# A transformer layer on one core: the tail of the token stage in a new order, and two edits ahead of it

## The reference

```python
x = x + attn(layernorm(x))     # Nystrom attention, 16 heads of 64, 64 landmarks, 6 pseudo-inverse rounds,
                               # a 13-tap convolution along the tokens, output weights w_fc, bias b_fc
x = x + moe(layernorm(x))      # sparsemixer router, top 2 of 8 experts, hidden size 512
...
sim1, sim2, sim3 = q @ k_l.T, q_l @ k_l.T, q_l @ k.T
out = softmax(sim1) @ pinv(softmax(sim2)) @ (softmax(sim3) @ v)
out = out + conv(out)          # along tokens, one filter of 13 taps per head
out = out @ w_fc + b_fc
...
h = silu(x @ w_gate[e].T) * (x @ w_up[e].T)
out = out + dense_w[:, e:e+1] * (h @ w_down[e].T)
```

## Time and profile before

| | us |
|---|---|
| median of 3 runs | 1186.02 (1185.68 to 1186.12) |
| profiled execution, whole | 1188.56 |
| its span, first to last instruction | 1186.8 |
| TensorE busy in it | 1122.7 (95%) |
| VectorE, ScalarE, GpSimd busy | 571.7, 301.7, 301.8 |
| mean granted TensorE clock | 0.991 of full speed |

### The profile page before, as it was taken

How to read it: one execution, slowest core, us unless ns; L and a number is a source line. 1 busy time by engine, 2 the same in 40 slices (tenths; PEclk the granted TensorE clock), 3 DMA queues, 4 the chain that set the end, 5 groups by cost and what they waited for, 6 DMA issues and landing times.

```text
span 1186.8 us, 22648 instructions
## 1 busy us (share of the span) xinstructions
PE 1122.7 (95%) x9066; PEld 886.9 (75%) x9066; DVE 571.7 (48%) x1273; ACT 301.7 (25%) x513; POOL 301.8 (25%) x298
## 2 busy tenths in 40 slices
PE   3999999999987899999999999878999999999997
PEld 3866667666776756677767766767888888899996
DVE  6254243232256557667777676654233323334442
ACT  4532222222223423223332332321111111111110
POOL 6000000000020003225435534443322332234343
PEclk9999999999999999999999999889999999999999
DMA  9300000000210030312321213235223332221221
GB/s 334 135 1 1 1 1 1 1 1 1 55 40 5 4 142 10 108 50 68 117 82 63 99 60 124 85 99 145 45 48 52 50 49 48 43 41 38 45 23 15
DMA packets 48551, 69.12 MB, mean 58 GB/s; under 512 B 7872, under 2 KB 41792, under 8 KB 47424
## 3 DMA queue, kind: packets, MB, share of 16 engines
q1 hardware_dynamic: 34720, 47.50, 12.5%
q0 software_dynamic: 13296, 16.92, 8.1%
q10 hardware_dynamic: 432, 3.24, 0.7%
HBM read 42.10 MB, written 26.46 MB: 58 GB/s over the span
## 4 chain that ended last, share of the span: by engine, by line
PE 89%; DVE 4%; issue 3%; POOL 1%; ACT 1%; another core or an unknown queue 1%; POOLq 0%; DVEq 0%; ACTq 0%
PE ps L1585 20%; PE ps L1608 10%; PE ps L1470 10%; PE ps L1268 9%; PE ps L1248 9%; PE ps L1509 9%; PE ps L1501 5%; PE ps L1259 3%; PE ps L1382 2%; PE ps L1211 1%; PE ps L1568 1%; PE ps L1489 1%; PE ps L1455 1%; PE ps L1223 1%
## 5 line engine op out<-in xcount | busy, mean ns | idle before, releaser
L1585 PE MATMUL ps<-mem 128*128 128x256 f32 (+1 forms) x1504 | 260.4, 329 | 0.0
L1585 PEld LDWEIGHTS ps<-mem 128*128 128x128 f32 x1504 | 232.6, 191 | 21.3
L554 POOL DMA_INDIRECT out<-mem x71 | 124.6, 1755 | 253.8 <-DVE mem L1130 188.0
L1608 PE MATMUL ps<-mem 128*128 x568 | 137.2, 385 | 5.0 <-DVE mem L1122 3.4
L524 POOL TENSOR_TENSOR mem<-mem,small 128x1024 f32<-128x1024 f32 x36 | 68.6, 1904 | 248.9 <-DVE small L1059 115.9
L1470 PE MATMUL ps<-mem 128*128 128x512 f32 x288 | 129.7, 594 | 1.3 <-DVE mem L943 1.3
L1122 DVE TENSOR_TENSOR mem<-mem,ps 128x512 f32<-128x512 f32 x71 | 48.8, 687 | 170.5 <-PE ps L1585 143.1
L742 ACT ACTIVATE mem<-ps 128x512 f32<-128x512 f32 x71 | 42.4, 597 | 322.6 <-PE ps L1585 315.8
L1509 PE MATMUL ps<-mem 128*128 128x256 f32 x512 | 119.7, 387 | 0.0
L1608 PEld LDWEIGHTS ps<-mem 128*128 128x128 f32 x568 | 105.6, 193 | 18.3 <-issue 5.7
L1248 PE MATMUL ps<-mem 128*128 128x512 f32 x256 | 115.4, 593 | 0.0
(11 more groups left out here) (205 smaller groups left out, 1316.2 us busy)
## 6 DMA issues: line engine op xcount, KB each, us to landing
mem<-w_gu SPq DMA_DIRECT2D x9, 1024.0 KB, 4.3
mem<-xs_d SPq DMA_DIRECT2D x22, 260.0 KB, 2.9
mem<-x SPq DMA_DIRECT2D x8, 512.0 KB, 7.4
mem<-x SPq DMA_DIRECT2D x32, 128.0 KB, 2.2
out<-mem SPq DMA_DIRECT2D x32, 128.0 KB, 1.7
mem<-w_down SPq DMA_DIRECT2D x8, 512.0 KB, 5.7
xnt_d<-mem ACTq DMA_DIRECT2D x3, 1056.0 KB, 4.4
mem<-xnt_d SPq DMA_DIRECT2D x3, 1056.0 KB, 4.9
```

The lines of the kernel that those rows point to most:

```text
L554: pool.indirect_dma_start(out=out_rows, out_offset=bass.IndirectOffsetOnAxis(ap=rows[:, D + 1:D + 2].bitcast(U32), axis=0), in_=ys[:, r % ...
L1585: mm = pe.matmul(bank(2 * c + n % 2)[:, i * size:(i + 1) * size], w[:, k, c, f * P:(f + 1) * P], xst[:, a % 2, k, 0:size], start=(k == 0), ...
L1608: mm = pe.matmul(bank(down_bank(a, b))[:, 0:D], hid[:, u, i * size + b * P:i * size + (b + 1) * P], w_d_s[:, e, f], start=(f == 0), stop=( ...
```

## The change

Five edits.

1. ACT_ROWS becomes a list per batch: ScalarE normalises tiles 3, 5, 7 of batches 0 and 1, tile 7 of batch 2 and none of batch 3. VectorE does the others. `act_rows` and `dve_rows` count them for the waits. ScalarE starts with a one-column ACTIVATE.
2. In batch 3 the last chunk's two products are copied out by VectorE, not by ScalarE.
3. The w_fc products of every second head pair are written to the opposite half of the output, so that a round's products use four quadrants, not two. The copy L943 reads them accordingly, and `c2_conv` places heads 2 and 3 of every four on opposite column halves, to match.
4. The tail's order on TensorE, ScalarE and VectorE. `x_columns(0)` moves into step 35, `hidden(0, 0)` and `hidden(1, 0)` in between the last convolutions; groups 6 to 8 are chosen and placed between the early items' work.
5. ScalarE gets two small ACTIVATEs of Exp in the tail (`exp_table`).

```diff
--- before.py
+++ after.py
-ACT_ROWS = (2, 5, 7)
+ACT_ROWS = ((3, 5, 7), (3, 5, 7), (7,), ())
...
+def act_rows(b, until=0):
+    return sum(len(rows) for rows in ACT_ROWS[:b]) + sum(t < until for t in ACT_ROWS[min(b, B - 1)])
+def dve_rows(b, until=0):
+    return RT * b + until - act_rows(b, until)
...
             act.wait_ge(s("a_consts"), 1)
+            act.activation(zz[:, 6:7], ident[:, 0:1], ACT.Identity, bias=ident[:, 1:2], scale=ident[:, 2:3])
...
-                for t in ACT_ROWS:
+                for t in ACT_ROWS[b]:
...
+                    if b == B - 1 and n == len(CHUNKS) - 1:
+                        act.wait_ge(s("a_xnt_dve"), 2 * KD)
+                        continue
...
-            for i in range(QT + 2):
+            def exp_table():
+                act.activation(zz[:, 7:8], zz[:, 1:2], ACT.Exp, scale=0.0)
+            for i in range(QT):
                 for h in range(2):
                     for g in groups_at(DONE, i - 2 - h):
                         if 2 * h < GROUPS[g][1]:
                             norm_columns(g, h)
-                if QT <= i < QT + 2:
-                    conv_out(i - 2)
                 for g in groups_at(CHOSEN, i - 1):
                     gap_exponentials(g)
                 for g in groups_at(DONE, i - 1):
                     for v in range(GROUPS[g][1]):
                         norm_rows(g, v)
-                if 2 <= i < QT:
+                if i >= 2:
                     conv_out(i - 2)
-                if i < QT:
-                    exponentials(i)
+                exponentials(i)
+            rows_transposed(0)
+            norm_columns(NG - 3, 0)
+            conv_out(QT - 2)
+            norm_columns(NG - 3, 1)
+            gate_out(0)
+            conv_out(QT - 1)
+            norm_rows(NG - 2, 0)
+            norm_rows(NG - 2, 1)
+            exp_table()
+            gap_exponentials(NG - 3)
             norm_columns(NG - 2, 0)
-            gap_exponentials(NG - 3)
-            rows_transposed(0)
             gap_exponentials(NG - 2)
-            gate_out(0)
+            gate_out(1)
+            rows_transposed(1)
             norm_rows(NG - 1, 0)
             norm_rows(NG - 1, 1)
-            gate_out(1)
             norm_columns(NG - 1, 0)
-            rows_transposed(1)
+            gate_out(2)
+            exp_table()
             gap_exponentials(NG - 1)
-            gate_out(2)
+            rows_transposed(2)
             gate_out(3)
-            rows_transposed(2)
             gate_out(4)
             rows_transposed(3)
...
+            ts = CHUNKS[-1]
+            for k in range(KD):
+                c = 6 * B - KD + k
+                dve.wait_ge(s("a_tp"), c + 1)
+                product = bank(c % 8)[:, 0:len(ts) * (P + RT)].rearrange("p (t c) -> p t c", t=len(ts))
+                at_ = HALO + P * ts[0]
+                dve.tensor_copy(xnts[B - 1][:, k, at_:at_ + P * len(ts)].rearrange("p (t c) -> p t c", t=len(ts)),
+                                product[:, :, 0:P]).then_inc(s("a_xnt_dve"), 1)
+                lm = M * (B - 1) + RT * ts[0]
+                dve.tensor_copy(xm[:, k, lm:lm + RT * len(ts)].rearrange("p (t c) -> p t c", t=len(ts)),
+                                product[:, :, P:P + RT]).then_inc(s("a_xnt_dve"), 1)
...
-                dve.tensor_copy(pm[:, g // 2, 4 * (g % 2):4 * (g % 2) + 4],
-                                bank(2 + 2 * (g % 2), 2).rearrange("p (s c) -> p s c", s=4)).then_inc(s("p_pm"), 1)
+                dve.tensor_copy(pm[:, g // 2, 4 * (g % 2):4 * (g % 2) + 4].rearrange("p (s o) c -> p o s c", o=2),
+                                bank(2 + 2 * (g % 2), 2).rearrange("p (o s c) -> p o s c", o=2, s=2)).then_inc(s("p_pm"), 1)
...
-            for i in range(QT + 4):
+            for i in range(QT + 1):
                 token_step(i)
+            rows_out(MT - 3)
+            statistics(MT - 3, NG - 2)
+            inverse_deviations(NG - 2)
             dve.wait_ge(s("c2_a1"), QT)
             hidden_out(0)
+            choices(NG - 3)
+            rows_out(MT - 2)
+            statistics(MT - 2, NG - 1)
+            slots(NG - 3)
+            choices(NG - 2)
+            rows_out(MT - 1)
+            statistics(MT - 1, NG - 1)
+            inverse_deviations(NG - 1)
+            hidden_out(1)
             slots(NG - 2)
-            hidden_out(1)
             choices(NG - 1)
+            rows_weighed(0)
+            hidden_out(2)
             slots(NG - 1)
             sizes()
             table(2 * P, 0, 8, NU, u_eid, u_row, "d_units")
-            hidden_out(2)
-            rows_weighed(0)
...
-                    for r in halves:
-                        mm = pe.matmul(bank(2 + 2 * (g % 2), 2)[r, i * D:(i + 1) * D], wts[r, g % 2, i], wfc[r, q % J],
-                                       start=True, stop=True)
+                    to = bank(2 + 2 * (g % 2) + i % 2)[:, i // 2 * D:(i // 2 + 1) * D]
+                    for h, r in enumerate(halves):
+                        mm = pe.matmul(to[halves[(h + i) % 2]], wts[r, g % 2, i], wfc[r, q % J], start=True, stop=True)
...
-                    c = 64 * (h % 2)
+                    c = 64 * ((h + h // 2) % 2)
...
+                if i == QT - 1:
+                    x_columns(0)
...
-            for i in range(QT + 2):
+            for i in range(QT):
                 token_step(i)
-            last = QT + 2
-            c2_tp(NG - 2, 0)
-            pe.wait_ge(s("c2_cvt"), cvt_count(QT - 1))
-            bank6_read(last)
-            c2_lg(NG - 2, 0)
-            c2_counts(NG - 3)
-            x_columns(0)
-            c2_y(MT - 1)
+            pe.wait_ge(s("m_xst"), 1)
+            c2_tp(NG - 3, 0)
+            c2_conv(QT - 2)
+            c2_lg(NG - 3, 0)
+            bank6_read(QT)
+            c2_y(MT - 3)
+            c2_tp(NG - 3, 1)
             pe.wait_ge(s("e_w_in"), 16)
             pe.wait_ge(s("c2_sub"), QT)
             hidden(0, 0)
             hidden(1, 0)
-            c2_counts(NG - 2)
+            c2_conv(QT - 1)
+            c2_lg(NG - 3, 1)
+            bank6_read(QT + 1)
+            c2_y(MT - 2)
+            c2_tp(NG - 2, 0)
+            c2_counts(NG - 3)
+            pe.wait_ge(s("c2_cvt"), cvt_count(QT - 1))
+            c2_lg(NG - 2, 0)
+            bank6_read(QT + 2)
+            c2_y(MT - 1)
             pe.wait_ge(s("d_taken"), NG - 2)
             hidden(0, 1)
             hidden(1, 1)
+            c2_counts(NG - 2)
+            x_columns(1)
+            pe.wait_ge(s("wd_in"), 16 * E)
+            pe.wait_ge(s("c2_x1"), MT)
+            down(0)
+            pe.wait_ge(s("m_xst"), 2)
             c2_tp(NG - 1, 0)
-            pe.wait_ge(s("wd_in"), 16 * E)
-            down(0)
+            down(1)
             pe.wait_ge(s("d_taken"), NG - 1)
             c2_lg(NG - 1, 0)
-            x_columns(1)
-            down(1)
-            c2_counts(NG - 1)
             hidden(0, 2)
             hidden(1, 2)
+            c2_counts(NG - 1)
+            x_columns(2)
             hidden(0, 3)
-            x_columns(2)
+            hidden(1, 3)
             down(2)
-            hidden(1, 3)
             hidden(0, 4)
             down(3)
             hidden(1, 4)
```

More of the change, by code:

```diff
@@ L344, in _ @@
                          router_t.rearrange("(k p) e -> p k e", p=P)).then_inc(s("w_in"), 16)
-            sp.wait_ge(s("a_xn_dve"), (RT - len(ACT_ROWS)) * (B - 1))
-            sp.wait_ge(s("a_xn_act"), len(ACT_ROWS) * (B - 1))
+            sp.wait_ge(s("a_xn_dve"), dve_rows(B - 1))
+            sp.wait_ge(s("a_xn_act"), act_rows(B - 1))
             sp.dma_start(wfc, w_fc.rearrange("(j p) c -> p j c", p=P)).then_inc(s("w_in"), 16)
@@ L594, in columns_out @@
                 if b >= 1:
-                    act.wait_ge(s("a_xnt"), 12 * (b + 1))
+                    act.wait_ge(s("a_xnt"), 12 * (b + 1) - (2 * KD if b == B - 1 else 0))
                     act.dma_start(xnt_d[b].rearrange("p (k n) -> p k n", k=KD), xnts[b]).then_inc(s("a_xnt_out"), 16)
@@ L801, in normalise @@
                 for t in range(RT):
-                    if t not in ACT_ROWS:
+                    if t not in ACT_ROWS[b]:
                         dve.tensor_scalar(xna[:, b, t], xbs[b][:, t], mv[:, b, t, 0:1], rs[:, b, t:t + 1],
@@ L1203, in _ @@
                 for n, ts in enumerate(CHUNKS):
-                    pe.wait_ge(s("a_xn_dve"), (RT - len(ACT_ROWS)) * b + sum(t not in ACT_ROWS and t <= ts[-1] for t in range(RT)))
-                    pe.wait_ge(s("a_xn_act"), len(ACT_ROWS) * b + sum(t <= ts[-1] for t in ACT_ROWS))
+                    pe.wait_ge(s("a_xn_dve"), dve_rows(b, ts[-1] + 1))
+                    if act_rows(b, ts[-1] + 1):
+                        pe.wait_ge(s("a_xn_act"), act_rows(b, ts[-1] + 1))
                     for k in range(KD):
@@ L1213, in _ @@
                         mm.then_inc(s("a_tp"), 1)
-            pe.wait_ge(s("a_xnt"), 12 * B)
+            pe.wait_ge(s("a_xnt"), 12 * B - 2 * KD)
+            pe.wait_ge(s("a_xnt_dve"), 2 * KD)
```

(52 more changed lines are left out.)

## The result

The changed kernel took 1176.53 us in the median of 4 runs (1175.75 to 1181.21), the kernel before 1186.07 beside it (4 runs). The ratio is 0.9927, with a 95% interval of 0.990 to 0.9954. The forecast was 1164.1, in 1159 to 1172. The kernel is faster, by 9.5 us and not by 22.

What follows compares the result with a forecast made beforehand. TensorE, busy 1122.7 of 1186.8 us, was taken as the bound, gaining only where it waits or its products run slow. Savings of 4.0, 6.9 and 11 sum to 21.9: 1164.1 against a median of 1186.02, range 1159 to 1172.

Steps and rivals of the forecast that it cites:

- The first stage: Start of the kernel: moving ScalarE's rows and last copies to VectorE saves 4.0 us, range 3.0 to 4.4.
- The quadrants: Output-weight rounds: four quadrants run together, halving 1.77 us per round, 0.87 saved in each of eight rounds, 6.9.
- rival B: Output-weight rounds: quadrants don't overlap in the w_fc products, so only 15.0 us saved, 1171; chance 0.10.
- rivals E and F: Convolutions: E, halves in strict program order, 8 us, chance 0.05; F, pair's heads run serially, 65 more, chance 0.03.
- The tail: Token stage's end to expert stage's start: new order saves 11 us, between 4 and 16 by late signals returning.
- With two fifths, 5 us: **11: Tail: two fifths of the 12.1 us of late signals return, costing 5 us, so 11 is saved.
- late signals: Tail: three waits, 12.1 us in all, with unknown releaser, after TensorE's product had ended, while GpSimd scatters rows.
- rival C: Tail: the late signals return in full, so 14.9 us saved in all, 1171; chance 0.15.
- The working without late signals: Tail: regular expert items start at 802.2 instead of 818.34, 16 us saved if no signal is late.
- VectorE's list: Tail: VectorE sets the end after the change; its work there, without waits, takes 40.9 us.
- first fixed point: Tail: VectorE's `rows_out` at 756.76, released by GpSimd's bias, which the change doesn't move.
- Terms 1 and 2: First stage, 4.0 us saved by moved rows and copies; output-weight rounds, 6.9 us saved by four quadrants.

Runs made afterwards that it cites:

- e2: Kernel before with only the w_fc products in four quadrants and the convolution's halves in the new order: 1179.8 us, ratio 0.9949.
- e12: The changed kernel again, unchanged, on another chip: 1173.1 us, ratio 0.9904.
- e3: Kernel before with only the tail's new order and the two small Exp ACTIVATEs: 1183.5 us, ratio 0.9987.
- e9: Changed kernel with one semaphore increment and wait on GpSimd behind each scatter of all groups: 1172.7 us, ratio 0.9892.
- e14: Changed kernel with four pairs of semaphore increment and wait on GpSimd behind each scatter of groups 5 to 8: 1175.0 us, ratio 0.9915.
- e1: Kernel before with only the first stage's rows and last copies moved from ScalarE to VectorE: 1182.7 us, ratio 0.9968.
- e11: Kernel before with one semaphore increment and wait on GpSimd behind each scatter of all groups: 1187.5 us, ratio 1.0009.
- e17: Kernel before with the first-stage and quadrant edits, tail in its old order, repeated on another chip: 1171.1 us, ratio 0.9903.
- e18: The changed kernel again, unchanged, on a chip without held signals: 1168.8 us, ratio 0.9881.
- e6_pauses_all: Changed kernel with eight pairs of semaphore increment and wait on GpSimd behind each scatter of groups 5 to 8: 1164.2 us, ratio 0.9858.
- e10: Changed kernel with eight semaphore increments and no wait on GpSimd behind each scatter of groups 5 to 8: 1169.9 us, ratio 0.9864.
- e13: Changed kernel with 14 semaphore increments and no wait on GpSimd behind each scatter of groups 5 to 8: 1170.7 us, ratio 0.9878.
- e8: Kernel before with the first-stage and quadrant edits, tail in its old order, no pauses: 1171.8 us, ratio 0.9907.
- e5: Changed kernel with eight pairs of semaphore increment and wait on GpSimd behind each scatter of groups 6 to 8: 1166.4 us, ratio 0.9874.
- e7: Kernel before with first-stage and quadrant edits, old tail order, eight increment-and-wait pairs behind each scatter of groups 6 to 8: 1169.1 us, ratio 0.989.
- e15: Kernel before with eight pairs of semaphore increment and wait on GpSimd behind each scatter of groups 5 to 8: 1186.0 us, ratio 0.9998.
- e16: Changed kernel with eight increment-and-wait pairs behind every scatter and every addition of rows in the expert stage: 1173.0 us, ratio 0.9895.
- e4: Changed kernel with one more GpSimd sum of 0.73 us into unused memory behind each scatter of groups 6 to 8: 1173.6 us, ratio 0.9902.

## Why the prediction was wrong

**The first stage** was right: 4.36 against 4.0. TensorE's start gave 0.8, the rest is ScalarE's rows and the last copies.

**The quadrants** were right, in size and in reason: 0.86 per round, eight rounds, 6.86 against 6.9. Two quadrants that read through the same half of the array do overlap with 256 columns too; rival B falls. The convolution stayed at 1.81 in after and e2, so rivals E and F fall. From the rule of the Trainium skill, page "TensorE: Matmul & The Clock Gate", section "Part 3: Packing small matmuls", that MATMULs start and end strictly in program order, I had worked out the loss of a slot at each repeated half; the page doesn't state that loss, and this trace shows none. One of my reasons was weaker than it looked. Products of two lines start between each other in the pseudo-inverse because the program's loop calls them in turn, which says little of quadrants. In the trace of before their records start at most 0.13 us out of that order.

**The tail** is where it failed, at the sentence "With two fifths, 5 us: **11**". In the profiled execution all of the late signals returned, and more: 12.1 before, 15.0 after. That is rival C, at 0.15, and the result lies beyond even that. In e12, the same kernel, 7.2 stood and the tail was 440.5, still only 5.6 under that of before. The working without late signals was close: 16 saved from a tail of 446.1 is 430.1, and the tails with the new order and nothing held are 432.4, 432.3 and 433.4. Of that 16, though, 12.1 was never the order's to give. Old tails with nothing held are 434.9, 436.6 and 439.5, 4.3 more in the mean than the new ones; the forecast's own difference, 16 - 12.1, is 3.9. Nor does the time of late signals seem all lost: on the two chips without them the kernel before is only 3 to 4.5 faster, not 12, though it was not profiled there. Where signals are held, as in the runs that the forecast was made against, the new order shows 439.9 to 446.6 (after, e3, e9, e12, e14), the old one 441.0 to 446.1 (before, e1, e2, e11). The means are 441.9 and 444.2, with spreads of 5 to 7. So where signals are held the orders differ by 2.3, less than either spread; e3, the order alone, won 3.0 in the medians and 1.5 by the ratio, and its interval takes in no change. Of the reasons that I gave for a smaller share, "early items give TensorE work ahead of the points that wait" didn't carry. In after TensorE did its two `down` and then stood for 6.9, as the logits behind them wait for ScalarE, and ScalarE for the signal that was held. The signals of both `down`, one ahead of the transposes and one behind, came out together with theirs (779.8 to 780.65), so work placed around a held signal didn't shorten the hold. And the pause brought the lower clock, which my sum left to the range.

**VectorE's list** was near. The waits of VectorE in after, from 749.5 to 811, stand against the earlier trace rows; the first is the logits' product, late by the hold:

```profile
DVE mem L1016 <- PE ps L1535: 10.7, 1, 10.7
DVE mem L1155 <- issue: 2.8, 1, 2.8
...
DVE mem L1016 <- remote: 1.8, 1, 1.8
```

The work itself was near the forecast: 61.9 from its first fixed point, less the 18.2 of waits listed for it, is 43.7, and I had 40.9, with 1.15 for a register load and an issue gap. My count of TensorE's products up to group 8's logits was a slip: its parts add up to 29.4 and not 28.9, which makes 0.5. ScalarE's two extra table loads were hidden: the list of VectorE's waits in after names ScalarE nowhere.

**The sum.** Terms 1 and 2 give 11.2. The change won 13.2 on the chip of e17 and e18. On chips that hold signals it won 9.5 (the result) and 11.8 (e12), so there the tail gave between -1.7 and 0.6 where 11 was forecast, with the pseudo-inverse's scatter in it. The range of 1159 to 1172 was too narrow on this side. It took the holds as known from one execution. The kernel before alone spreads over 1178 to 1192 in 81 runs beside e1 to e18.

**The best version** so far is e6_pauses_all with 1164.2, 0.9858 of before, on a chip without held signals. After stands at 0.9881 on the other such chip, and the intervals overlap. Where signals are held, e10 and e13 (0.9864, 0.9878) stand under after (0.9904, 0.9927).

## What to carry to other kernels

A stall whose releaser the profile can't name doesn't belong to the order of the work. If its cause isn't known, forecast the gain once with it back in full and once without it, and keep both in the range. Sort a saving into what the edit does and what it hopes will vanish: here the first was 3.9 of 16. And run a control on the same chip before crediting a cure: e8 showed that e5 to e7 were no evidence of one.

## What the runs showed of the hardware that I had not expected

- TensorE's semaphore updates can arrive up to 10 us after its product's record has ended (10.4 in e11), while GpSimd issues scatters without a pause, and then several arrive together: in after those of two `down` and the transposes, ended at 769.8, 774.4 and 772.0, were visible at 779.8, 780.65 and 780.6. No update of VectorE or ScalarE was over 0.6 us late between 440 and 830 in any of the twenty traces.
- It depends on the chip, or on something else that stays the same for a set of runs. In two sets of five no trace shows it, with the same kernels and the same scatters 1.27 apart; the kernel before is 3 to 4.5 us faster there (1182 against 1185 to 1186). The chip that ran two sets, half an hour apart, held signals in both.
- On the others no signal was held for groups 6 to 8 when increments spread the scatters to 1.6 to 2.1 apart (14 of them, 1.65 us of GpSimd's sequencer for each scatter, e13) or sums did (1.9 to 2.9 apart, e4). With eight pairs (1.33 us, scatters 1.3 to 1.4 apart, e15 and e16) signals were still up to 3.5 late. Whether the sequencer's time or the rate of the scatters decides is not shown.
- A sum on GpSimd between scatters lengthened VectorE's work by a fifth (44.4 against 36.6 us for 171 instructions).
